# Two 32x32 block transposes on VectorE for the division of the contexts

## The reference, cut to what matters

```python
scores = jnp.einsum('bhqd,bhkd->bhqk', q, k) * SCALING + position_bias
attn = jax.nn.softmax(scores, axis=-1)
ctx = jnp.einsum('bhqk,bhkd->bhqd', attn, v)      # 16 heads of 8 features
x = x + ga * (ctx @ Wo.T)
...                                               # second attention, then experts
```

## Time and profile before

| | |
|---|---|
| median of 3 runs | 1079.14 us |
| the profiled execution's own time | 1078.02 us |
| its span, first to last instruction | 1076.2 us |
| PE busy | 925.0 us (86%) |
| DVE busy | 696.7 us (65%) |
| ACT busy | 481.0 us (45%) |
| POOL busy | 201.8 us (19%) |
| granted TensorE clock, mean | 0.96 of full speed |

### The profile page before, as it was taken

How to read it: one execution, slowest core, us unless ns; L and a number is a source line. 1 busy time by engine, 2 the same in 40 slices (tenths; PEclk the granted TensorE clock), 3 DMA queues, 4 the chain that set the end, 5 groups by cost and what they waited for, 6 DMA issues and landing times.

```text
span 1076.2 us, 39365 instructions
## 1 busy us (share of the span) xinstructions
PE 925.0 (86%) x16386; PEld 610.7 (57%) x16386; DVE 696.7 (65%) x1464; ACT 481.0 (45%) x814; POOL 201.8 (19%) x244
## 2 busy tenths in 40 slices
PE   4787899998999999899998989999999979888841
PEld 2445465565656556565654656666566757666730
DVE  1564677777686777768678776677686464656623
ACT  1343455545555554555554445555455434333310
POOL 1340021202111220211112020201110010155225
PEclk9887899999999999999999999999999999999985
DMA  7389100000000000000000000000001011134313
GB/s 223 140 316 386 54 9 16 17 7 18 7 23 8 17 18 7 17 8 22 7 18 17 23 26 13 27 18 22 28 24 35 26 40 37 48 109 135 93 47 91
DMA packets 50299, 59.08 MB, mean 55 GB/s; under 512 B 6672, under 2 KB 37392, under 8 KB 49744
## 3 DMA queue, kind: packets, MB, share of 16 engines
q1 hardware_dynamic: 36272, 28.24, 8.5%
q10 hardware_dynamic: 9760, 19.92, 5.0%
q0 software_dynamic: 4096, 8.40, 2.7%
HBM read 22.92 MB, written 33.62 MB: 53 GB/s over the span
## 4 chain that ended last, share of the span: by engine, by line
PE 74%; DVE 11%; issue 6%; ACT 4%; DMA 2%; POOL 2%; SPq 1%; POOLq 0%; DVEq 0%; ACTq 0%
PE ps L792 9%; DVE row_max L1155 6%; PE ps L893 6%; PE ps L648 6%; PE ps L885 5%; PE ps L681 5%; PE ps L659 5%; PE ps L693 5%; PE ps L638 3%; ACT probs L992 3%; PE ps L816 3%; PE ps L887 3%; PE ps L639 3%; PE ps L623 3%; PE ps L629 3%
## 5 line engine op out<-in xcount | busy, mean ns | idle before, releaser
L1155 DVE TENSOR_REDUCE row_max<-ps 128x4 f32<-128x1024 f32 (+1 forms) x256 | 271.8, 1087 | 83.0 <-PE ps L659 50.6
L992 ACT ACTIVATE probs<-ps 128x1024 f32<-128x1024 f32 x128 | 130.5, 1024 | 84.8 <-PE ps L681 82.3
L992 ACT ACTIVATE stage<-ps 128x1024 f32<-128x1024 f32 x96 | 98.1, 1024 | 85.9 <-PE ps L687 85.2
L885 PE MATMUL ps<-xT_t,wgu_hi 128*128 128x128 f16 x480 | 101.7, 225 | 33.5 <-issue 31.2
L648 PE MATMUL ps<-bias_t,ch 64*32 64x512 f16 x2048 | 109.8, 392 | 13.4 <-DVE q_rows L1172 6.2
L1375 POOL TENSOR_TENSOR rstd_n<-var_n,cf 128x2 f32<-128x2 f32 x48 | 34.0, 709 | 453.1 <-DVE var_n L1084 453.1
L1306 DVE SCALAR_TENSOR_TENSOR gate_s<-gate_t,ps 128x256 f32<-128x256 f32 x120 | 50.2, 418 | 79.1 <-ACT gate_t L1042 73.3
L886 PE MATMUL ps<-xT_t,wgu_hi 128*128 128x128 f16 x480 | 99.0, 219 | 0.0
L887 PE MATMUL ps<-xT_t,wgu_lo 128*128 128x128 f16 x480 | 98.9, 219 | 0.0
L1042 ACT ACTIVATE gate_t<-ps 128x256 f32<-128x256 f32 x120 | 46.1, 384 | 107.2 <-PE ps L887 93.3
L792 PE MATMUL ps<-probs,v_pad 128*32 128x256 f32 x1024 | 83.6, 398 | 4.6 <-ACT probs L992 3.8
(11 more groups left out here) (171 smaller groups left out, 1810.3 us busy)
## 6 DMA issues: line engine op xcount, KB each, us to landing
slot_rows<-gate_s ACTq DMA_DIRECT2D x1, 12032.0 KB, 35.6
slot_rows<-gate_s ACTq DMA_DIRECT2D x1, 7424.0 KB, 31.3
x_t<-slot_rows SPq DMA_DIRECT2D x80, 64.0 KB, 1.9
slot_rows<-eo_t SPq DMA_DIRECT2D x80, 64.0 KB
xT<-in_x SPq DMA_DIRECT2D x16, 128.0 KB, 2.0
kept<-resid SPq DMA_DIRECT2D x16, 128.0 KB, 1.8
resid_b<-kept SPq DMA_DIRECT2D x16, 128.0 KB, 2.5
out_dram<-outT SPq DMA_DIRECT2D x16, 128.0 KB, 2.0
```

The costliest lines, as they stand in the source:

```text
L885: eng.matmul(dst, wgu_hi[:, w, block], x_hi, start=True, stop=False)
L992: eng.activation(probs[a][:, 2 * (k % 2):2 * (k % 2) + 2, :], ps[:, lo:lo + 2, :], ACT.Exp).then_inc(z["exp"], 1)
L1155: ins = eng.tensor_reduce(row_max[a][:, qt, 4 * g:4 * g + 4].rearrange("p (r j) -> p r j", r=2), of_heads, AX.X, ALU.max)
```

## The change

The two ones columns in `v_pad` become four (columns 16 to 19 alternate between the two heads), so bank `X` holds each denominator twice. DVE then does the division alone: a 32x32 block transpose of the bank to `ctx_sb` (`byq`, queries on partitions), reciprocals of the four denominator columns of each block (`rec`), a second block transpose that reads each reciprocal 8 times (`byd`), and a product of the bank with `ctx_sb` (`ctxn`). The steps `ctx` and `wide` of ACT and `den` and `div` of PE are gone, with their wait in front of the second Exp. Bank `X` is given back after `ctxn` and no longer after the copy.

```diff
-        last = self.op((job, i, "ctx"), "act", 0.60, [("c%d" % a, i, "end")] + self.before(job, i), (), X)
-        last = self.chain(job, i, last, ("den", "pe", 0.9, SHARED), ("rec", "dve", 0.56, (), "mine"), ("wide", "act", 0.6),
-                          ("div", "pe", 0.9, SHARED), ("ctxn", "dve", 0.69, (), "mine"))
+        last = self.op((job, i, "byq"), "dve", 0.62, [("c%d" % a, i, "end")] + self.before(job, i))
+        last = self.chain(job, i, last, ("rec", "dve", 0.56), ("byd", "dve", 0.62), ("ctxn", "dve", 0.69, (), X))
...
+            eng.transpose(ctx_sb[a][:, :, :].rearrange("p r s -> p (r s)"), ps[:, X, :]).then_inc(z["byq"], 1)
...
+            eng.reciprocal(rden[a][:, :].rearrange("p (n k) -> p n k", k=4), by_block[:, :, 16:20]).then_inc(z["rec"], 1)
...
+            eng.transpose(ctx_sb[a][:, :, :].rearrange("p r (n d) -> p (r n) d", d=HD),
+                          rden[a][:, :].unsqueeze(2).to_broadcast([P, 64, HD])).then_inc(z["byd"], 1)
...
+            eng.tensor_tensor(ctx_sb[a][:, :, :], ps[:, X, :].rearrange("p (r s) -> p r s", r=2), ctx_sb[a][:, :, :],
                               ALU.mult).then_inc(z["ctxn"], 1)
```

```diff
-GAP = {"pe": 0.0, "act": 0.03, "dve": 0.03, "pool": 0.05, "sp": 0.1}
+GAP = {"pe": 0.0, "act": -0.09, "dve": -0.08, "pool": 0.05, "sp": 0.1}
...
-                self.op(key + ("pe",), "pe", 0.66, before + xt, banks)
+                self.op(key + ("pe",), "pe", 1.0 if c else 2.2, before + xt, banks)
```

More of the change, by code:

```diff
@@ L40 @@
 for _n, _w in (("ident", P), ("cos", S), ("sin", S),
-               ("den_sel", 16), ("kmask", HJ), ("kones", HJ), ("expert", NX), ("tri", NX * NX), ("tile", T_MAX),
+               ("kmask", HJ), ("kones", HJ), ("expert", NX), ("tri", NX * NX), ("tile", T_MAX),
                ("first", len(PARTS) * NX), ("zero", 1), ("half", 1)):
@@ L169, in core @@
             if sid[0] == "e":
-                pe = self.op((job, i, sid), "pe", 0.46, [pe], CORE, mode=1)
-                self.op((job, i, "x%d" % k), "act", 1.05, [pe] + ([(job, i, "c%d" % (k - 2))] if k > 1 else [])
-                        + ([("b%d" % a, i - 1, "div")] if i and k == 1 else []), (), "mine")
+                pe = self.op((job, i, sid), "pe", 0.44 if a == 1 or len(PAIRS[a][k][1]) > 1 or not PAIRS[a][k][0] else 0.33, [pe], CORE, mode=1)
+                self.op((job, i, "x%d" % k), "act", 1.05, [pe] + ([(job, i, "c%d" % (k - 2))] if k > 1 else []), (), "mine")
             else:
-                pe = self.op((job, i, sid), "pe", 0.57, [pe, (job, i, "x%d" % k)] + ([(job, i, "vz")] if not k else []),
+                pe = self.op((job, i, sid), "pe", 0.45, [pe, (job, i, "x%d" % k)] + ([(job, i, "vz")] if not k else []),
                              (X,) if not k else (), mode=2)
@@ L531, in block_kernel @@
         att = {a: signals("a%d_" % a, "mean xc qk v hi vz lo kspread qspread krow khead qrow score max "
-                          "mxhi mxlo maxt qmax wscore exp pv ctx den rec wide spread ctxn o") for a in (1, 2)}
+                          "mxhi mxlo maxt qmax wscore exp pv byq rec byd ctxn o") for a in (1, 2)}
         x1_done, h2_done = sem("x1_done"), sem("h2_done")
@@ L579, in given_back @@
                 return (x1_done if job == "b1" else h2_done), i + 1
-            return {"mean": z["xc"], "qk": z["lo"], "v": z["vz"], "c0": z["ctx"], "den": z["rec"], "div": z["ctxn"],
+            return {"mean": z["xc"], "qk": z["lo"], "v": z["vz"], "c0": z["ctxn"],
                     "mx": z["maxt"], "mxrows": z["qmax"]}[name], i + 1
@@ L799, in pe_back @@
             job, z = "b%d" % a, att[a]
[L800 to L817, removed]
             yield at("out")
@@ L1176, in dve_back @@
             z, job = att[a], "b%d" % a
-            yield at("rec")
-            eng.wait_ge(z["den"], i + 1)
-            eng.reciprocal(rden[a][:, :], held(job, i, "den")[:, 0:64]).then_inc(z["rec"], 1)
+            by_block = ctx_sb[a][:, :, :].rearrange("p r (n m) -> p (r n) m", m=HR)
+            yield at("byq")
+            eng.wait_ge(z["pv"], n_u[a] * (i + 1))
+            if i:
+                eng.wait_ge(z["o"], i)
+            eng.transpose(ctx_sb[a][:, :, :].rearrange("p r s -> p (r s)"), ps[:, X, :]).then_inc(z["byq"], 1)
+            yield at("rec")
+            eng.wait_ge(z["byq"], i + 1)
+            eng.reciprocal(rden[a][:, :].rearrange("p (n k) -> p n k", k=4), by_block[:, :, 16:20]).then_inc(z["rec"], 1)
+            yield at("byd")
+            eng.wait_ge(z["rec"], i + 1)
+            eng.transpose(ctx_sb[a][:, :, :].rearrange("p r (n d) -> p (r n) d", d=HD),
+                          rden[a][:, :].unsqueeze(2).to_broadcast([P, 64, HD])).then_inc(z["byd"], 1)
             yield at("ctxn")
-            eng.wait_ge(z["spread"], i + 1)
-            eng.tensor_tensor(ctx_sb[a][:, :, :], ctx_sb[a][:, :, :], held(job, i, "div").rearrange("p (r s) -> p r s", r=2),
+            eng.wait_ge(z["byd"], i + 1)
+            eng.tensor_tensor(ctx_sb[a][:, :, :], ps[:, X, :].rearrange("p (r s) -> p r s", r=2), ctx_sb[a][:, :, :],
                               ALU.mult).then_inc(z["ctxn"], 1)
@@ L1346, in pool_fill @@
             for e in range(2):
[L1347 removed]
+                ones = v_pad[a].rearrange("p k (r i c) m -> p (k r) i c m", r=2, i=2)[:, :, e, :, 16 + e:20 + e:2]
                 ins = eng.memset(ones, 1.0)
@@ L1531, in _ @@
             act_setup(eng)
-            weave([f(eng, i) for f in (act_f1, act_b1, act_f2, act_b2, act_h) for i in range(B)]
+            weave([f(eng, i) for f in (act_f1, act_f2, act_b2, act_h) for i in range(B)]
                   + [f(eng, a, i) for f in (act_values, act_core) for a in (1, 2) for i in range(B)] + [act_moe(eng)])
```

30 lines of the change are left out of this document (4 added, 26 removed).

## The result

The changed kernel takes 1100.58 us (median of 4 runs, 1099.38 to 1104.11), the kernel before, on the same chip, 1078.06 (1076.76 to 1079.93): ratio 1.0213, 95% interval 1.0189 to 1.0237. It is slower, and 0.6 us beyond the end of my range. The profiled execution took 1104.11 us with a span of 1102.3.

A forecast was written before the change was run, and what follows sets the result against it. PE sets the pace, DVE one step behind in a loop. Second part's start +0.4, half clock +3 and finals -1.6 gave +1.8: span 1076.2 to 1078.0, forecast 1080 us after run offsets, range 1060 to 1100.

The forecast's parts named there:

- Removed and added work: Each period: 3.58 us of `den` and `div` leave PE, four transposes of 0.60 us come to DVE.
- Rival C: Slower: a transpose costs what a maximum costs, 1.22 us, adding 23 us: 1103 us; chance 0.10.
- Steady stretch: 205 to 592 us: new PE idle offsets removed PE work, so eight periods change by 0, from -10 to +8 us.
- I take 47.0: Predicted steady period in us, unchanged from before, within some 1 us a period.
- +4.35 us idle: New PE idle per steady period from waits for DVE at two places: 1.45 + 1.2 + 1.7.
- -3.58: PE work in us leaving each steady period, from two `den` (0.99, 0.81) and two `div` (0.89 each).
- Start-up: Five contexts alone on the chain get shorter: 4 us gained, from 0 to 8, so image 10 comes earlier.
- Places A and B: PE waits before weight tiles: attention 2, 2.3 us idle, then about 1.2 more; attention 1, 2.4 idle.
- Mixed stretch: Up to the last `out`: -19.7 us PE work, +34.3 experts moved ahead, +3 uncovered chain, -3 filler; `out` ends at 916.9.
- Hole: Last `out` to second part's first `gu`: 27.3 us with almost no PE work, then half clock losing 3 us.
- slower: Outcome class for the whole kernel, above the no-change band of 1075.9 to 1082.4 us; chance 0.40.

The follow-up runs named there:

- x5: The changed kernel's operations in another order, set by cost-table numbers for maximum, weight tile, value product, first transpose and key heads: 1061.42 us, ratio 0.9847.
- x10: The changed kernel with one cost-table number changed, TensorE's mode switch planned at 0.200 us instead of 0.095: 1069.8 us, ratio 0.9922.
- x3: The changed kernel with the planned duration of `gu` back at 0.66 us: 1083.6 us, ratio 1.0049.
- x1: The changed kernel with the cost-table numbers of the kernel before, new operations kept: 1089.47 us, ratio 1.0101.
- x2: The kernel before with the cost-table numbers of the changed kernel, old operations kept: 1091.97 us, ratio 1.0119.
- x9: The kernel before in its own order, with eleven extra VectorE writes of attention 2's maxima for each image: 1138.22 us, ratio 1.0561.
- x7: The operations of the kernel before (`den`, `div`, copies) in another order, set by cost-table numbers: 1059.61 us, ratio 0.9821.
- x8: The kernel before in its own order, with four extra VectorE writes of attention 2's maxima for each image: 1089.76 us, ratio 1.0094.

## Why the prediction was wrong

- **Removed and added work: right.** `den` and `div` went; in orders without dips PE's period is 40.15 to 40.8 us busy, 40.2 predicted. A transpose is 0.71 us (0.68). Rival C came near the time (1103) with a mechanism that did not happen. The Trainium skill's 0.69 ("VectorE: DVE Perf Modes", the section on the TRN2 errata) is stated there for an fp32 tensor_tensor add, so it was an estimate by analogy; the trace has 0.70 to 0.71 for the transposes. That page's section "The DRAIN you can't avoid", which I said the trace contradicts, goes on that a next operation that is not held starts earlier; the trace fits that, with 0.62 to 0.64 us from a transpose to the next start.
- **Steady stretch: the step that failed.** "I take 47.0" was +4.35 us idle against -3.58, so 0 for eight periods, and it was +13.7. Over eight periods PE's idle time rose from 29.5 to 51.9 us, 22.4 or 2.8 a period, even less than the 4.35. What failed is the -3.58: PE's busy time fell by 8.6 us (347.28 to 338.64) instead of 28.6. I had counted PE's work at full clock because the clock read 1.00 in the earlier trace rows, and had never asked what the new gaps would do to it, though the earlier trace rows showed half clock after a pause and I used them for the hole. Of the missing 20 us, half clock accounts for at most 12 ((30.7 - 6.8)/2); an estimate without the dips is thus 390.5 - 12, near 379 us, inside my range for the stretch. The other 8 are 1.0 a period: the changed order's period without a dip has 41.33 busy for 40.2 (with five products more in its window than x5's); x10's has 40.80, x5's 40.19, so this also hangs on the order, but its cause stays open.

The trace of the kernel before already held the warning. From 592 us on it shows one cluster behind which PE, without a gap, ran at half clock:

```profile
639.33 0.23 PE L885 MATMUL ps<-xT_t,wgu_hi 128*128 128x128 f16 x1 [1.01 <-issue]
...
642.22 0.41 PE L659 MATMUL ps<-stage 64*32 64x512 f16 x8 [1.03 <-DVE row_max L1155]
...
643.35 0.41 PE L648 MATMUL ps<-bias_t,ch 64*32 64x512 f16 x8 [0.61 <-DVE row_max L1155]
```

```profile
640.00:644.00 4.00, 2.36 (x82) 1.09 (x84) 3.06 (x3) 0.39 (x1) 0.00 (x0) 1.00 0.06 19
644.00:648.00 4.00, 4.00 (x43) 2.45 (x44) 3.04 (x9) 2.50 (x3) 0.00 (x0) 0.57 0.01 4
```

- **Start-up: -4 was right to image 0 only** (-5.7). Then images 0 to 2 gave 4.6 back, with 28.0 us at half speed, so that at image 2 only 1.1 of the 4 was left.
- **Places A and B: right.** 1.87 and 1.09 idle at A for 2.3 and 1.2; at B 0.66 + 1.36 + 0.42 = 2.44 in the period from 509.59 for 2.4.
- **Mixed stretch: the direction right, 4.6 us short.** All experts went in front of the last `out`. Idle rose by 8.8 us (23.2 to 32.0), where I had 3 more and 3 less; PE's busy time rose by 10.4 (286.2 to 296.7), where I had 14.6 (-19.7 + 34.3), so two errors partly cancel. x3 shows that this term hangs on the planned `gu` by 9 us.
- **Hole: 30.3 for 27.3.** The fourth scatter ended 23.3 us after `out` (22.2 predicted). From the end of that scatter to `tr` it was 4.0 (3.9). From `tr` to `gu` it was 3.05 for 1.2, with a final and its wait in between: that is 1.85 of the 3. The clock in it was 0.50, as said, and the stretch after it 133.8 to the tenth.
- **The chances.** I gave 0.40 to slower, most of it for a wrong reason. A rival "the gaps lower the clock" was missing, and with it the range was too short above. That the miss of the range is only 0.6 us is no merit of the sum.

## What to carry to other kernels

Read PE's busy time as work divided by clock: when a change moves short gaps of PE together, ask what the granted clock did behind such a cluster elsewhere in the trace, and price half clock on the work that stands behind the gaps. In a kernel whose order comes from a cost table, an edit that touches the table is two changes; run each alone (x1, x2) before the operation gets the blame or the praise. And when both variants can be reordered, compare each in a good order: here 1.7 us a context less on PE was worth nothing in the orders tried, a number for the mode switch 31 us.

## What the runs showed of the hardware

- The granted clock fell to 0.50 in the middle of a stretch in which PE was over 85% busy: behind gaps of 0.78, 0.54, 0.55 and 1.09 us (changed kernel), of 0.72, 0.61, 0.61 and 0.61 us (x2), of 2.05, 0.51 and 0.59 us (x9, eight times of nine), and once of only 0.36, 0.61 and 0.64 us (x7). It stayed at 1.00 behind 0.51 and 0.59 (x8), and where ten gaps with 5.75 us in all were spread over 46 us, the closest large ones 0.60 and 1.36 us, 3.3 us apart (x5, images 2 to 9). What exactly decides is not shown. DVE and ACT instructions kept their durations in the dips (a 128x1024 maximum 1.18 to 1.23 us, an Exp of 128x1024 1.02).
- Two periods of x9 with equal gaps in front differ in having the dip, and between the changed kernel and x3 dips came at other images in a stretch whose order is the same. That orders with dips are less even from run to run is not shown: the changed kernel spreads over 4.7 us in four runs, x1, with more half-speed time in the steady stretch, over 2.0, and x5, with hardly any there, over 5.4.
- A 128x512 fp32 block transpose on VectorE takes 0.71 us from PSUM and 0.70 us from SBUF with a broadcast input, 0.62 to 0.64 us from its start to the start of the next one.
